# Five batch chunks of 256, 512, 512, 512 and 256 rows in place of four of 512, in a feature-interaction kernel

## The reference: what is computed

```python
p = feat_emb[:, rows, :]
q = feat_emb[:, cols, :]
pij = jnp.einsum('bpe,dpe,bpd->bp', p, kernel, q)
z = pij @ W.T + b
h = jnp.concatenate([z, dense_ctx], axis=1)
h = jnp.maximum(h @ W_top1 + b_top1, 0.0)
h = jnp.maximum(h @ W_top2 + b_top2, 0.0)
y = h @ W_top3
```

## Time and profile before

| | |
|---|---|
| median of 3 runs | 797.37 us (796.73 to 798.46) |
| profiled execution | 796.73 us, its span 794.9 us, 1.8 us less |
| PE / DVE / ACT / POOL busy | 760.8 / 623.9 / 551.3 / 472.3 us |

### The profile page before, as it was taken

One profiled execution on the slowest core, in us unless ns is written; L12 is line 12 of the kernel. 1 busy time (PEld: TensorE's weight loads), 2 busy tenths in 40 slices (PEclk: granted clock), 3 DMA queues, 4 the chain that ended last, 5 costly groups with the idle time before them and its releaser, 6 DMA issues.

```text
span 794.9 us, 29641 instructions
## 1 busy us (share of the span) xinstructions
PE 760.8 (96%) x11784; PEld 283.7 (36%) x11784; DVE 623.9 (78%) x580; ACT 551.3 (69%) x4181; POOL 472.3 (59%) x502
## 2 busy tenths in 40 slices
PE   3989899999989999999999999999999999999998
PEld 0323233344333333333333333333333333333333
DVE  4577789999957677999957677999984768999950
ACT  0100599999935687999914587999932668999942
POOL 5777777777777777777777777777777500000000
PEclk9999999999999999999999999999999999999999
DMA  9911111111111111111111111111111100000000
GB/s 248 376 56 28 28 29 30 29 29 29 29 30 28 28 28 29 30 29 30 28 31 28 28 29 28 29 30 29 30 29 29 22 2 3 2 3 3 3 3 0
DMA packets 21681, 30.50 MB, mean 38 GB/s; under 512 B 10898, under 2 KB 11410, under 8 KB 20904
## 3 DMA queue, kind: packets, MB, share of 16 engines
q0 software_dynamic: 15872, 16.28, 10.6%
q1 hardware_dynamic: 3512, 9.58, 3.4%
q10 hardware_dynamic: 2160, 2.76, 1.3%
HBM read 28.58 MB, written 0.01 MB: 36 GB/s over the span
## 4 chain that ended last, share of the span: by engine, by line
PE 72%; POOL 9%; issue 6%; DVE 5%; ACT 5%; DMA 1%; SPq 1%; DVEq 0%; POOLq 0%
PE bilinear L699 30%; PE sums L741 16%; PE bilinear L713 12%; PE bilinear L783 11%; POOL emb L440 5%; ACT batch_prod L525 5%; POOL emb_first L440 4%; PE bilinear L676 3%; DVE prod L595 3%; DVE prod L592 1%; DVE batch_prod L606 1%; PE sums L725 1%; SPq L410 1%; DMA sums_sb<-dense_t 1%; ACT emb_t L484 0%
## 5 line engine op out<-in xcount | busy, mean ns | idle before, releaser
L525 ACT ACTIVATE batch_prod<-batch_prod 128x64 f32<-128x64 f32 x2048 | 489.2, 244 | 17.6 <-DVE batch_prod L606 17.6
L595 DVE TENSOR_TENSOR prod<-bilinear,emb_t 128x1024 f32<-128x1024 f32 x352 | 416.1, 1217 | 101.5 <-PE bilinear L699 99.5
L440 POOL DMA_INDIRECT emb<-table,ids_sb x368 | 347.4, 944 | 112.1 <-issue 109.4
L525 ACT ACTIVATION_READ_ACCUMULATOR batch_prod<-batch_prod 128x1 f32 x2048 | 389.9, 190 | 0.0
L699 PE MATMUL bilinear<-emb_t,k_sb 64*32 64x512 f32 x5888 | 368.1, 594 | 4.3 <-DVE prod L592 3.4
L741 PE MATMUL sums<-prod,row_sel 64*32 64x512 f32 x2944 | 196.8, 590 | 0.7 <-DVE prod L595 0.7
L699 PEld LDWEIGHTS bilinear<-emb_t,k_sb 64*32 64x32 f32 x5888 | 110.0, 107 | 207.1 <-issue 151.0
L606 DVE TENSOR_TENSOR batch_prod<-bilinear,emb_first 128x1024 f32<-128x1024 f32 x128 | 155.7, 1217 | 14.7 <-PE bilinear L713 13.7
L440 POOL DMA_INDIRECT emb_first<-table,ids_sb x128 | 124.2, 971 | 44.6 <-issue 37.0
L713 PE MATMUL bilinear<-k_sb,emb_t 64*32 64x512 f32 x2048 | 137.1, 590 | 1.1 <-DVE prod L592 1.1
L484 ACT ACTIVATE emb_t<-bilinear 128x1024 f32<-128x1024 f32 (+1 forms) x40 | 34.0, 851 | 96.7 <-PE bilinear L676 90.0
(11 more groups left out here) (29 smaller groups left out, 102.6 us busy)
## 6 DMA issues: line engine op xcount, KB each, us to landing
emb<-table,ids_sb POOLq DMA_INDIRECT x368, 2.5
emb_first<-table,ids_sb POOLq DMA_INDIRECT x128, 2.4
k_sb<-k_slots SPq DMA_DIRECT2D x2, 896.0 KB, 19.7
k_sb<-k_slots SPq DMA_DIRECT2D x1, 1600.0 KB, 23.1
k_sb<-k_slots SPq DMA_DIRECT2D x1, 1408.0 KB, 19.4
k_sb<-k_slots SPq DMA_DIRECT2D x1, 1088.0 KB, 16.4
sums_sb<-looked_ids SPq DMA_DIRECT2D x1, 1024.0 KB, 10.0
k_sb<-k_slots SPq DMA_DIRECT2D x1, 1024.0 KB, 26.5
```

Source lines behind the costliest of these rows:

```text
L440: nc.gpsimd.indirect_dma_start(fields_of(i, j, t)[:, f % 2, :], None, tables[f], bass.IndirectOffsetOnAxis(ap=ids_sb[:, start + t, f:f + 1 ...
L525: last = nc.scalar.activation(products, products, ACT.Copy, accum_out=batch_sums[:, t, half, row + f:row + f + 1])
L595: last = nc.vector.tensor_tensor(prod[:, at:at + 2, 0:n], bilinear[:, bank:bank + 2, 0:n], emb_t[:, j:j + 1, 0:n].to_broadcast([P, 2, n]), ...
```

## The change

The first and the last chunk have half the rows, and there is one chunk more. Batches in the short chunks are set twice as far apart in slots. The look-up works on 256 rows.

```diff
-CHUNK_TILES = (4, 4, 4, 4)
+CHUNK_TILES = (2, 4, 4, 4, 2)
@@ units
-    after = [start + n * every for n in range(len(batches))]
+    after = [start + n * every * max(CHUNK_TILES) / tiles for n in range(len(batches))]
@@ build
-        looked_ids_sb = sums_sb[:, 0:2 * LOOKED_UP, :].bitcast(i32)
+        looked_ids_sb = sums_sb[:, 0:2 * LOOKED_UP, 0:CHUNK_TILES[0] * P].bitcast(i32)
@@ one-hot on DVE
-                    nc.vector.tensor_scalar(one_hot[:, at:at + 2, :], looked_ids_sb[:, 2 * j:2 * j + 2, :],
+                    nc.vector.tensor_scalar(one_hot[:, at:at + 2, 0:cols(0)], looked_ids_sb[:, 2 * j:2 * j + 2, :],
@@ look_up on PE
-                            last = nc.tensor.matmul(bilinear[col:col + QUARTER, bank, :],
+                            last = nc.tensor.matmul(bilinear[col:col + QUARTER, bank, 0:cols(0)],
                                                     tables_sb[0:parts, f, k, e:e + QUARTER],
-                                                    one_hot[0:parts, n % ONE_HOT_RING * 2 + c, :],
+                                                    one_hot[0:parts, n % ONE_HOT_RING * 2 + c, 0:cols(0)],
```

## The result

Five runs of the changed kernel gave a median of 827.34 us (825.94 to 829.37), against 797.37 us before. The ratio is 1.0373, with a 95% interval of 1.0356 to 1.0391: 3.7% slower. The forecast was 816.5 us, slower by 2.4%, in a range of 808 to 828 over all its cases and of 808 to 825 for the forecast itself. The profiled execution of after took 829.4 us, its span is 827.3, so on spans the change costs 32.4 us and the forecast of 814.4 is 12.9 short. It was the longest of the five; the spans of the other four are 823.8 to 825.7, and on medians the change costs 30.0 us and the forecast is 10.8 short.

What follows compares the result with a forecast made beforehand. PE bounds the kernel, except at the start, where POOL is just early enough. Turn of 6 and 7 at 166.5, 321.3 next, two chunks to 689.3, plus 59.5, 47.5 and tail 18.1: span 814.4, forecast 816.5 us; range 808 to 828.

Steps and rivals of the forecast that it cites:

- the rival in which POOL slips further: In chunk 0 POOL and PE wait for each other turn after turn, losing 4 to 10 us more: 820 to 827; 8%.
- POOL's pause: In chunk 0, gather 21 waits until PE has turned double 4, at 40.0: 4.5 us lost, bounds 0 to 8.
- POOL's rule: Gather n lands at 28.10 + 1.2486 (n - 15) + 2.5 us, POOL pacing itself whatever PE does.
- Part 1, the start: Look-up of 19.6 us about halves; first turn at 34.3 instead of 43.77; chunk 0 ends between 120 and 130.
- Part 2, from the turn of 4 and 5 to that of 6 and 7: In the second chunk, PE goes on at 146.2 when gather 104 lands and reaches the turn of 6 and 7 at 166.5.
- some 36 us: Time from about 130 to 166 in which PE was said to have nothing to turn, set against the gains.
- The list of signs: What the trace would show, such as PE idle before line 676 some 35 us between 105 and 167.
- the rival that takes it away: POOL's 0.30 us of issue is slack, so second-chunk gathers come with PE: 26 us lower, 790; 5%.
- Part 3: From the turn of 6 and 7 to the end: 321.3, two full chunks of 184.0, last slot 796.3, tail 18.1.
- Half price for short units: A PE slot, sum or batch of 256 columns steps by 0.43 us, against 0.86 at 512.
- I add 3.0 of its 4.2 us: Last chunk, up to the turn of 12 and 13: gaps of 3.0 us on 56.5 of counted work, giving 59.5.
- the 0.9 us for two engines that don't mesh: Last chunk, to its last slot: PE and DVE each have 46.6 us of work, taken as 47.5.

Runs made afterwards that it cites:

- experiment 6: Changed kernel with the looked-up ids packed, so that their load lands in pieces of 4 KB instead of 1 KB: 823.3 us.
- experiment 3: Changed kernel without POOL's waits on turns in the first chunk (LEAD_FROM 16 instead of 7): 814.1 us.
- experiment 1: Changed kernel with 48 plain DMAs on SP replacing POOL's gathers of doubles 0 to 5 of the second chunk: 805.3 us.
- experiment 5: Changed kernel with 48 plain DMAs for gathers, DVE's short-chunk slot products halved: 803.4 us; last chunk's batch products halved too: that chunk 108.7 us, from 113.7.
- experiment 2: Kernel before, with 48 plain DMAs replacing POOL's gathers of doubles 0 to 5 of the second chunk: 796.3 us.
- experiment 8: Kernel before, with a chunk's first two layers after slots 7 and 10 instead of 5 and 8: median 792.54 us, ratio 0.9926.

## Why the prediction was right, and where it was off

**In short.** The direction and the mechanism held: the second chunk's gathers come too late for the halved work ahead of them, PE stands for them, and the whole gain of the start is lost there. The size was off: 19.1 us slower were forecast, 30.0 measured. The forecast's own range, to 825, was missed by 2.3 us. That 827.34 lies below 828 is luck: beyond 825 and near it only the rival in which POOL slips further had a time (820 to 827), and this didn't happen. The terms that were too small are the last chunk (6.7 us), POOL's pause (2.1 by its effect), the stretch behind the wait (2.0) and the clock in the third chunk (1.8). The sum itself has a slip of 0.3: 816.2 and 0.6 are 816.8, not 816.5.

**What bounds the kernel, and POOL's rule.** Right. 1.2486 us a gather and 2.5 to landing held after the change too; counted from the real end of POOL's pause it gives 42.16 + 83 x 1.2486 + 2.5 = 148.3 for gather 104, which is to the tenth where PE goes on.

**Part 1, the start.** The first turn came at 37.0 and not 34.3. I had the look-up begin no later than before; it began at 13.89 in place of 12.41, since the load of half the bytes lands later when it comes in pieces of 1 KB (experiment 6), and it took 10.8 us, not 9.8. The sentence that all in chunk 0 is covered by the wait failed here: the late look-up moved the turn of double 4, and so the end of POOL's pause.

**Part 2, POOL's pause.** Mis-sized: 4.5 us said, 9.1 measured (10.34 from gather 20 to 21, less 1.25), outside my bounds of 0 to 8. Half of it is that gather 21 was due at 33.1 and not 35.6, since POOL's early gathers ran faster (gather 20 at 31.82, where before it was at 34.34), half that turn 4 came at 41.45 and not 40.0, and the gather 0.7 behind it. What counts for the end is only the second half: gather 104 landed 2.1 us later than said. The rival in which POOL slips further, by turn after turn, didn't happen; there was one pause, at 33 us and not near 36.

**Part 2, from the turn of 4 and 5 to that of 6 and 7.** 22.3 us for 20.3. I allowed 1.7 us for a slower clock; the stages show 0.52 from 133 to 154 us and 0.58 again from 164 to 168. This stretch isn't the same from run to run: 20.8 us in experiment 6, 21.3 in experiment 3. Together the turn came at 170.6 for 166.5: 4.1 of the 12.9 us.

My sentence that PE has nothing to turn for "some 36 us" was wrong as a size of the loss, though no term of the sum used it: nine slots of the second chunk and a layer lie in that time. The list of signs says it again, with some 35 us idle before line 676; the trace has 16.7. The wait costs 20.0 (experiment 1), and the rival that takes it away was put at 26.

**Part 3.** To the end of the second chunk 155.2 for 154.8, right, though two terms offset: the halved layers gave 7.7 of the 8.6 us counted (162.8 to 155.2), and the wait of 0.6 for gather 152 didn't come. Two full chunks took 369.8 for 368.0: 186.0, with the slow clock from 342 to 346 us, and 183.7.

**The last chunk.** 113.7 for 107, 6.7 of the 12.9 us and the largest miss. Half price for short units was right to 0.01 us. The sustained figures of the Trainium skill ("TensorE: Matmul & The Clock Gate", Back-to-back issue gap) don't hold for these units: by the estimate made from them, three quarters of 0.86, a short one would take 0.65, and it was measured at 0.43. What failed is the sentence on the gaps, "I add 3.0 of its 4.2 us", and the 0.9 us for two engines that don't mesh. Gaps didn't halve with the columns here. In the first part the stage is 63.9 us long for 56.5 us of counted work, so its gaps grew from 4.2 to 7.4 us; the dense rows' wait alone took 2.35. The second part took 49.8 for 47.5. New gaps appear where work of full width stands between short units (5.0 us over both parts by experiment 5).

**The tail.** 18.1, as said.

**Where the expected gain went.** Without the gathers' wait the split still costs 10.4 us. From the starts of the turns: start 6.3 and tail 13.1 gained; the four chunks took 170.8 + 184.1 + 184.0 + 181.0 = 719.9 before, the five now 93.6 + 174.7 + 184.1 + 183.6 + 113.5 = 749.5, so 29.6 lost. About 10 of these are no loss but the tail's own layers, which now stand ahead of it in PE's queue: PE's work was moved, not removed. The others, some 20, are the two short chunks over half of the full ones (85.4, and 101.9 with full layers and join). Of them 5.0 are shown as the batches' latency in the last chunk; that the rest is other fixed latencies (a turn's way over ACT, changes of shape on PE) was only argued. How the loss divides between start and first chunk is soft: in two more runs that begin as before the first turn came at 45.7, 1.9 us later (experiments 2 and 8), and the turn of 4 and 5 at 214.5 and 214.9 all the same, since the first chunk there waits for its own gathers (1.01, 2.30 and 0.63 us before).

## What to carry to other kernels

Halving the first piece of work halves the time in which a slow, even supplier can run ahead; compare for each later consumer its place in the supplier's queue with the work that now stands before it, and count a pause of the supplier as a delay of the end where a later consumer waits for it. On an engine that is 96% busy a shorter tail is worth only its idle time where, as here, its work goes elsewhere in the same queue. Half the width doesn't halve latencies, and a ring of buffers that covered a full-width product is short when the units around it shrink.

## What the runs showed of the hardware that was not expected

- A load of 512 KB in pieces of 1 KB took 12.0 us to land, one of 1024 KB in pieces of 8 KB 10.0 us at the same place of the queue, and the 512 KB in pieces of 4 KB 8.5 us (the first two in the traces of after and before; others of their kind are in experiment 6, the last is one trace).
- After waits of 7.58 and 8.85 us with little between them, the granted clock stayed at its lower level for 6 us of dense work (to 154 us). It isn't the same from run to run: behind the same wait of about 2 us for the dense rows in the third chunk it fell after the change (0.57 from 342 to 346 us, the chunk 186.0 us) and didn't before (184.0), and with experiment 2's edit on the kernel before it fell there again (0.72 from 412 to 418 us, the chunk 185.9).
